# Recurrent stage as one block of 256 half-steps, and attention rows laid in another order

## The reference, cut to what matters

```python
def step(h, x_t):
    proj = h @ W
    score = jnp.einsum('bsh,bh->bs', enc_hiddens, proj)
    attn = jax.nn.softmax(score, axis=-1)
    context = jnp.einsum('bs,bsh->bh', attn, enc_hiddens)
    inp = jnp.concatenate([x_t, context], axis=-1)
    gx = inp @ kernel + bias
    gh = h @ recurrent_kernel
    ...
    z = jax.nn.sigmoid(xz + hz)
    r = jax.nn.sigmoid(xr + hr)
    cand = jnp.tanh(xh + r * hh)
    h_new = z * h + (1.0 - z) * cand
    return (h_new, h_new)
```

```python
def _attn(q, k, v, mask):
    scores = jnp.einsum('bqhd,bkhd->bhqk', q, k) / np.float32(np.sqrt(HD))
    scores = jnp.where(mask[:, None, None, :], jnp.float32(-jnp.inf), scores)
    w = jax.nn.softmax(scores, axis=-1)
    return jnp.einsum('bhqk,bkhd->bqhd', w, v)
```

## Time and profile before

| what | value |
|---|---|
| median of 3 runs | 7409.12 us (7405.55 to 7414.10) |
| profiled execution, its own time | 7413.49 us |
| its span | 7411.7 us |
| instructions | 189154 |
| busy share of the span | PE 80%, PEld 59%, DVE 65%, ACT 39%, POOL 14% |
| granted clock of TensorE, mean | 0.843 |

### The profile page before, as it was taken

The page is one execution under the profiler, slowest core; times in us unless marked ns, Lnnn a source line. Parts: engine busy times, 40 slices in busy tenths (PEclk is TensorE's granted clock), DMA queues, the critical chain, the costliest instruction groups (busy, mean ns, idle before and its releaser), DMA issues. The chain is left out here.

```text
span 7411.7 us, 189154 instructions
## 1 busy us (share of the span) xinstructions
PE 5923.4 (80%) x79720; PEld 4340.8 (59%) x79720; DVE 4782.4 (65%) x16863; ACT 2871.5 (39%) x4943; POOL 1039.1 (14%) x930
## 2 busy tenths in 40 slices
PE   4454569888888788888799788888888888888887
PEld 3343446666566577777677456556555565565565
DVE  6767964544558766666544676675775765775764
ACT  2221224444434311111111256455554554664563
POOL 1113522212210200000000210111111111011101
PEclk7666778998989755555699899999999989999998
DMA  1000000000000000000000000000000000000000
GB/s 34 1 0 3 1 30 1 1 1 1 1 5 2 6 3 3 3 3 4 25 1 1 19 2 2 11 2 3 10 2 7 6 2 11 2 2 11 2 2 15
DMA packets 61221, 44.63 MB, mean 6 GB/s; under 512 B 22521, under 2 KB 56125, under 8 KB 60227
## 3 DMA queue, kind: packets, MB, share of 16 engines
q1 hardware_dynamic: 51817, 26.98, 1.4%
q10 hardware_dynamic: 8538, 5.27, 0.2%
HBM read 30.14 MB, written 2.10 MB: 4 GB/s over the span
## 5 line engine op out<-in xcount | busy, mean ns | idle before, releaser
L262 DVE TENSOR_REDUCE peak<-ps 128x8 f32<-128x1024 f32 (+1 forms) x832 | 817.0, 1024 | 259.2 <-PE ps L184 258.5
L304 ACT ACTIVATE e<-ps,H_lowT_s 128x1024 f32<-128x1024 f32 x384 | 407.0, 1111 | 250.6 <-PE ps L208 250.6
L304 ACT ACTIVATE e<-ps,H_lowT_c 77x1024 f32<-77x1024 f32 x384 | 405.5, 1105 | 252.7 <-PE ps L208 252.7
L222 PEld LDWEIGHTS ps<-e,H_vt 128*32 128x32 f32 (+1 forms) x12288 | 320.3, 112 | 256.7 <-ACT e L304 140.3
L222 PE MATMUL ps<-e,H_vt 128*32 128x128 f32 (+1 forms) x12288 | 433.7, 282 | 23.6 <-DVE xs L282 17.8
L2486 POOL TENSOR_TENSOR H_rstd<-H_veps,neghalf 128x4 f32<-128x4 f32 (+1 forms) x148 | 161.7, 1093 | 1994.6 <-DVE H_veps L2482 1994.6
L208 PE MATMUL ps<-H_qr,H_km 32*128 32x128 f32 (+1 forms) x12288 | 426.4, 277 | 0.0
L208 PEld LDWEIGHTS ps<-H_qr,H_km 32*128 32x128 f32 (+1 forms) x12288 | 412.2, 171 | 15.6 <-issue 2.0
L312 ACT ACTIVATE oT<-ps 128x512 f32<-128x512 f32 x416 | 248.4, 597 | 353.9 <-PE ps L222 353.9
L2178 ACT ACTIVATE F_rz<-F_gsum 128x32 f32<-128x32 f32 x256 | 58.6, 229 | 822.7 <-DVE F_gsum L2116 822.7
L184 PE MATMUL ps<-H_km,H_qr 32*128 32x512 f32 (+1 forms) x3072 | 348.3, 520 | 0.0
(11 more groups left out here) (638 smaller groups left out, 13777.5 us busy)
## 6 DMA issues: line engine op xcount, KB each, us to landing
H_f<-in_L_xcond_f_w SPq DMA_DIRECT2D x12, 256.0 KB
H_nw<-in_L_xcond_n_w SPq DMA_DIRECT2D x21, 128.0 KB, 2.1
A_cond<-in_cond ACTq DMA_DIRECT2D x1, 2048.0 KB, 11.6
G_w<-in_L_ffn_w SPq DMA_DIRECT2D x8, 256.0 KB
G_w<-in_L_ffn_w ACTq DMA_DIRECT2D x8, 256.0 KB, 8.2
out_x<-x_all SPq DMA_DIRECT2D x1, 2048.0 KB, 8.7
ctx_rows<-in_ctx SPq DMA_DIRECT2D x1, 1232.0 KB
D_wq<-in_L_xcond_attn_wq SPq DMA_DIRECT2D x2, 512.0 KB
```

The source lines that it names most:

```text
L222: last = nc.tensor.matmul(ps[PAD_COLS * s:PAD_COLS * (s + 1), FLAT, r * S:(r + 1) * S], vt_of(u)[0:keys, QUAD * r + s, :], e[0:keys, half, ...
L262: last = nc.vector.tensor_reduce(peak[:, HL * half:HL * (half + 1)], view, AX.X, ALU.max, negate=True)
L304: nc.scalar.activation(e[0:keys, half, :], ps[0:keys, AGAIN[half]:AGAIN[half] + 2, :].rearrange("p b t -> p (b t)"), ACT.Exp, bias=low(u) ...
```

## The change

In the recurrent stage the loop is gone. One block holds all 256 half-steps. `hist` has 129 steps and takes the place of `gru`, which leaves, as do the two token copies with their two waits in the gate sums, the copy of the state and the scaling of the states. The gate sums read `tok` itself. The initial state is written at step 0 of `hist`. The transposes read `hist`, and the additions to `x_all` multiply by the factor on the way.

In the helper, `scores` lays the rows of groups 2 and 3 after the wait for `peaks_ready` and ahead of the wait for `exp_done`, and those of groups 0 and 1 behind it. `again` lays its bias rows in the order 2, 3, 0, 1, after the waits for `shift_ready` and `exp_done`; the wait for `half_peaked` now stands between the rows of group 3 and of group 0. The order of the products behind them is as before.

```diff
+            def lay_low(u, groups):
+                for r in groups:
+                    nc.tensor.matmul(view(r), ones_b[ROWS * r:ROWS * r + 1, :], ... start=True, stop=False, skip_group_check=True)
             def scores(u):
                 N = first + u
                 ready(u)
                 if N >= 1:
                     pe.wait_ge(sem["peaks_ready"], N)
+                if low_of:
+                    lay_low(u, (2, 3))
                 if N >= 2:
                     pe.wait_ge(sem["exp_done"], 2 * N - 3)
                 if low_of:
-                    for r in range(QUAD):
-                        nc.tensor.matmul(view(r), ...)
+                    lay_low(u, (0, 1))
...
             def again(u):
                 pe.wait_ge(sem["shift_ready"], N + 1)
-                if u + 1 < units:
-                    pe.wait_ge(sem["half_peaked"], N + 2)
                 if N >= 1:
                     pe.wait_ge(sem["exp_done"], 2 * N)
-                for r in range(QUAD):
+                for r in (2, 3, 0, 1):
+                    if r == 0 and u + 1 < units:
+                        pe.wait_ge(sem["half_peaked"], N + 2)
                     nc.tensor.matmul(ps[0:keys, bank(r), :]..., start=True, stop=False, skip_group_check=True)
...
-            RUN = 32
-                gru = sb("F_gru", [D, S, B], scope=st)
-                PART = RUN // 2
-                xloc = [...]
-                hist = sb("F_hist", [D, RUN + 1, B], scope=st)
+                hist = sb("F_hist", [D, S + 1, B], scope=st)
...
-                HALVES = CH * RUN
-                with nc.Fori(0, S // RUN) as n:
-                    with nc.Block() as block:
+                HALVES = CH * S
+                with nc.Block() as block:
...
-                            step(nc.vector.tensor_copy(hist[:, 0, :], hist[:, RUN, :]))
...
                             def gate_sums(k):
-                                if k == 0:
-                                    dve.wait_ge(sem["x_ready"], 1)
-                                if k == CH * PART:
-                                    dve.wait_ge(sem["later_ready"], 1)
                                 dve.wait_ge(sem["gate_done"], k + 1)
-                                nc.vector.tensor_tensor(gsum[:, c], ps[...], xloc[t // PART][:, t % PART, :, mine(c)], ALU.add)
+                                nc.vector.tensor_tensor(gsum[:, c], ps[...], tok[:, t, :, mine(c)], ALU.add)
...
-                            dve.wait_ge(sem["h_low"], HALVES)
-                            nc.vector.tensor_scalar(gru[:, bass.ds(n * RUN, RUN), :], hist[:, 1:RUN + 1, :], unscale[:, STATE:STATE + 1], None, ALU.mult)
-                        @block.gpsimd
-                        def _(pool):
-                            nc.gpsimd.tensor_copy(xloc[0], tok[:, bass.ds(n * RUN, PART)]).then_inc(sem["x_ready"], 1)
-                            nc.gpsimd.tensor_copy(xloc[1], tok[:, bass.ds(n * RUN + PART, PART)]).then_inc(sem["later_ready"], 1)
...
-                                last = nc.tensor.transpose(ps[...], gru[:, :, i * U + u], ident[:])
+                                last = nc.tensor.transpose(ps[...], hist[:, 1:S + 1, i * U + u], ident[:])
...
-                            nc.vector.tensor_tensor(x_all[...], x_all[...], per(i), ALU.add)
+                            nc.vector.scalar_tensor_tensor(out=x_all[...], in0=per(i), scalar=unscale[:, STATE:STATE + 1],
+                                                           in1=x_all[...], op0=ALU.mult, op1=ALU.add)
```

More of the change, by code:

```diff
@@ L168, in small_tensor @@
             rows = lambda r: slice(ROWS * r, ROWS * (r + 1))
+            view = lambda r: ps[:, r, :].rearrange("p (s k) -> p s k", s=QUAD)[:, :, 0:keys]
+            def lay_low(u, groups):
+                for r in groups:
+                    nc.tensor.matmul(view(r), ones_b[ROWS * r:ROWS * r + 1, :],
+                                     low_of(u)[ROWS * r:ROWS * r + 1, :].unsqueeze(1).broadcast_to([1, QUAD, keys]),
+                                     start=True, stop=False, skip_group_check=True)
             def scores(u):
@@ L174, in scores @@
                     pe.wait_ge(sem["peaks_ready"], N)
+                if low_of:
+                    lay_low(u, (2, 3))
                 if N >= 2:
                     pe.wait_ge(sem["exp_done"], 2 * N - 3)
-                view = lambda r: ps[:, r, :].rearrange("p (s k) -> p s k", s=QUAD)[:, :, 0:keys]
                 if low_of:
-                    for r in range(QUAD):
-                        nc.tensor.matmul(view(r), ones_b[ROWS * r:ROWS * r + 1, :],
-                                         low_of(u)[ROWS * r:ROWS * r + 1, :].unsqueeze(1).broadcast_to([1, QUAD, keys]),
-                                         start=True, stop=False, skip_group_check=True)
+                    lay_low(u, (0, 1))
                 for r in range(QUAD):
@@ L1827, in stage_gru @@
                 rstd_b = oT[:, 9 * B:10 * B]
-                gru = sb("F_gru", [D, S, B], scope=st)
-                PART = RUN // 2
-                xloc = [t.rearrange("p (t i b) -> p t i b", t=PART, i=3)
-                        for t in (pT[:].rearrange("p b h s -> p (b h s)")[:, 0:PART * 3 * B], e[:].rearrange("p b n -> p (b n)")[:, 0:PART * 3 * B])]
                 gsum = sb("F_gsum", [D, CH, 3, CB], scope=st)
@@ L1903, in _ @@
                         nc.vector.tensor_scalar(gate_w["h"][:], gate_w["h"][:], unscale[:, STATE:STATE + 1], None, ALU.mult)
-                        step(nc.vector.tensor_scalar(hist[:, RUN, :], condT[:], scale[:, STATE:STATE + 1], None, ALU.mult))
-                        step(nc.vector.tensor_copy(hp[:, :, 0], hist[:, RUN, :]))
-                        nc.vector.tensor_tensor(hp[:, :, 1], hist[:, RUN, :], hp[:, :, 0], ALU.subtract)
+                        step(nc.vector.tensor_scalar(hist[:, 0, :], condT[:], scale[:, STATE:STATE + 1], None, ALU.mult))
+                        step(nc.vector.tensor_copy(hp[:, :, 0], hist[:, 0, :]))
+                        nc.vector.tensor_tensor(hp[:, :, 1], hist[:, 0, :], hp[:, :, 0], ALU.subtract)
                         for n in ("c", "h"):
@@ L2194, in stage_gru @@
+                rest()
                 with nc.Block() as block:
@@ L2198, in _ @@
                             for u in range(U):
-                                last = nc.tensor.transpose(ps[:, i, u * D:(u + 1) * D], gru[:, :, i * U + u], ident[:])
+                                last = nc.tensor.transpose(ps[:, i, u * D:(u + 1) * D], hist[:, 1:S + 1, i * U + u], ident[:])
                             last.then_inc(sem["turned"], 1)
@@ L2205, in _ @@
                             dve.wait_ge(sem["turned"], i + 1)
-                            nc.vector.tensor_tensor(x_all[:, i * U:(i + 1) * U, :], x_all[:, i * U:(i + 1) * U, :], per(i), ALU.add)
+                            nc.vector.scalar_tensor_tensor(out=x_all[:, i * U:(i + 1) * U, :], in0=per(i), scalar=unscale[:, STATE:STATE + 1],
+                                                           in1=x_all[:, i * U:(i + 1) * U, :], op0=ALU.mult, op1=ALU.add)
                 rest()
```

307 lines of the change are left out of this document (153 added, 154 removed).

## The result

The changed kernel took 7326.73 us (median of 4 runs, 7319.35 to 7335.69), the kernel before 7411.61 (4 runs, 7405.55 to 7426.29): ratio 0.9878, 95% interval 0.986 to 0.9895, 85 us less. I had forecast 7370 (7345 to 7389), 39 less. The sign was right; the size was outside the range. The profiled execution took 7324.31 us, 89.2 less than that of before. In one later experiment ("half_peaked written first"), one of ten runs took 21442.3 us at a granted clock of 0.227, where the others had 0.840 to 0.845; it is left out of the median there.

The account below looks back on a forecast made before the run. No engine is full; a chain through engines sets the recurrent period, a path through ScalarE and TensorE attention. Terms -35.8 - 4 + 1 = -39 made 7374.5 us; that execution being 4.4 above the median, forecast 7370 (7345 to 7389).

Parts of the forecast that it names:

- Recurrent stage, -35.8: One block of 256 half-steps: boundary gaps go, -35.4 us; last scaling leaves, -0.9; additions with multiply, +0.5.
- Rivals C and D: Recurrent stage: C, long block outruns instruction supply, 7434, chance 0.04; D, period slower by 0.07 us, 7388, chance 0.05.
- So I take 0.01 us a unit, -4: Scores: rows 2 and 3 ahead of the exponential's wait save 0.01 us in 384 units; bounds -42 and +20.
- my reading of the slices: Scores: 0.02 us slices show all four row products starting together, so two rows fewer behind the wait save little.
- 0.07 us in 56 units: Second products ("again"): half_peaked's wait moves from its own queue entry to a weight load, -4 us.
- rival B: Both row splits: each costs a 51 ns queue entry on the path, 800 splits, 41 us, 7411, no change; chance 0.07.
- "again", net +1: Second products' new row order and wait, 416 units: gain of 4 us against loss of 4 to 7; bounds -12, +21.
- The loss of 4 to 7 us in the other 360: "Again": group of L208's first product laid third instead of first, 0.01 to 0.02 us in each of 360 units.
- Rival A: Attention: rows cost their issue, so each taken off the path gives its time; 7320, half of it 7345; chance 0.09.
- attention units shorter by 0.1 us (A): Sign the forecast was wrong: attention unit periods, expected the same within 0.03 us, shrinking by 0.1 us would show rival A.
- L184 closer than 0.21 us: Sign the forecast was wrong: score products (L184) were expected still 0.21 us after the second pair of L180 rows.
- some 5 us either way: TensorE's lower-clock spells may fall elsewhere once everything behind 3610 us comes earlier; some 5 us, inside the range.

Follow-up runs that it names:

- half_peaked written first: Kernel before, with only the half_peaked wait in the second products moved ahead of those for shift_ready and exp_done; median 7.9 us less, ratio 0.9988.
- the run that kept the entry: Kernel before, scores' rows 2 and 3 laid ahead, the pair behind keeping both waits, peaks_ready and exp_done; 7407.6 against 7406.65 us.
- exp_done first: Kernel before, with only the exp_done wait in the scores written ahead of peaks_ready, no row moved; 7367.37 against 7406.65 us, ratio 0.994.
- the scores split: Kernel before, with only the scores' rows 2 and 3 laid ahead of the exp_done wait; median 24.0 us less, ratio 0.9957.

## Why the prediction was wrong

- **Recurrent stage, -35.8.** Right: 35.2 between the gate sums, 1049.6 us where 1049.4 were worked out; no gap, and SyncE's four waits over the stage became one. The additions take 740 to 753 ns each, as forecast. The end of the stage gave 1.1 where I had 0.4 (last gate sum to the end of the additions: 10.8 us before, 9.7 after). Rivals C and D are gone: the stage fetched 196 instruction packets, 203 before, and no two gate sums are more than 4.12 us apart, where before it was up to 16.2.
- **"So I take 0.01 us a unit, -4"**: this is the step that failed. As a price of laying rows it was right (0.005 and 0.0075 us by the run that kept the entry, 2.4 us in all), and my reading of the slices stands. But the edit did a second thing: it gave each of two waits an instruction of its own. I had noticed a change of carrier in "again" and priced it at 0.07 us in 56 units; in the scores, in 384 units on the path, I didn't ask who carried the exp_done wait. In rival B I even wrote that the number of waits doesn't grow; what counted was their place. The trace of before had the sign of it: the exponential ends at 4293.01 + 1.11 = 4294.12, the row starts only at 4294.26, 0.14 us later, with the entry between. The term measured -36.4 by the units, where its lower bound was -42 for another reason.
- **"again", net +1.** The units say -0.8 in 384 units, and the first attention stage gave 1.1 more (32 units of 5.046, now 5.013). The reason I gave for the gain, the carrier, is right: the run with half_peaked first has the same 5.013 with no row moved. But its size there is 0.03 us a unit, half of my 0.07. The loss of 4 to 7 us in the other 360 does not show: self-attention units became 0.0115 shorter, cross ones 0.0075 longer.
- **Rival A** had a time (7320) near the measured one and the wrong mechanism. My own marker, "attention units shorter by 0.1 us (A)", came out true for another reason, and so did "L184 closer than 0.21 us": the scores start 0.02 us behind the second pair but last 0.19 longer, so the path is no shorter for it. The run with the rows moved and the entry kept was needed to part them. A marker by period alone can't name its cause.
- **The clock, "some 5 us either way".** Too small. The profiled execution's 89.2 us are made up so. 37.2 lie ahead of the last attention stage's first exponential (4215.9 to 4178.7): 35.2 between the gate sums, 1.1 at the end of that stage, 1.1 in the first attention stage, less some tenths. 45.3 lie inside the twelve attentions, from first to last exponential of each (1949.7 to 1904.4 in sum): 36.2 are the shorter units (31 periods in each attention, so a little less than the 37.4 of 32), and 9.1 are starts that spend less time at the lower level. The last 6.7 lie between the attentions and behind them (1246.1 to 1239.4), where the clock also changes level; I can't place them. Why a variant gets more or fewer long starts is open: a shift of the stage in time may change them, but no run isolates it.

## What to carry to other kernels

Where an instruction on the path has several waits, look in the queue's records for a wait entry right behind the event that ends last: writing that wait first, or giving it an instruction of its own, gave 0.08 to 0.09 us each on TensorE, here 34 us for one moved line. Writing it last cost 0.06 us each on ScalarE. Before crediting a reordering with a gain, build the twin that moves the work and keeps the waits. And compare small changes by the period of a unit at one clock level; medians of whole runs differ here from the units by 10 us and more, a part of it through the clock.

## What the runs showed of the hardware that I had not expected

An entry that lasts 51 ns on TensorE costs 0.08 to 0.09 us when its wait ends last. When it passes early it costs nothing measurable: with exp_done first (402 entries) the unit is 5.2775 us, with the scores split and no entry ahead of the waiting pair 5.2730, and the 0.005 between them is what laying rows ahead is worth. On ScalarE an entry of 17 ns costs 0.06.

On TensorE the timelines split it. From the end of the exponential to the weights of the row it is 0.11 us before (4294.12 to 4294.23) and 0.06 with exp_done written first (4255.87 + 1.11 = 4256.98 to 4257.04), which is the entry. And before, the first product comes 0.03 us behind its weights, where now it comes with them. Over 192 units the medians are 112 and 51 ns for the first, 31 and 4 ns for the second: 0.061 + 0.027 = 0.088 us. With exp_done first:

```profile
4257.04 0.10 PEld L180 LDWEIGHTS ps<-H_low_s,ones_b 1*128 1x128 bf16 x4 [0.72 <-ACT e L304]
4257.04 0.40 PE L180 MATMUL ps<-H_low_s,ones_b 1*128 1x512 bf16 x4 [0.57 <-ACT e L304]
```

For ScalarE the 0.06 is more than the record, and nothing splits it.

Which wait goes where can be read, since the trace keeps the semaphores of every record: the wait written first rides on the instruction itself, and the others stand in entries ahead of it, up to two in one entry. So "again", with three waits, has one entry for two of them: half_peaked and exp_done before, shift_ready and exp_done with half_peaked written first. That entry lasts 592 ns in the median before and 51 after the swap, since the late wait has left it. In the scores one unit of four waits for tables and groups of keys as well and has two entries (90 of line 174 beside the 402 of line 176).
